# First layer norm of a Swin block without TensorE: 32x32 blocks transposed on VectorE, statistics spread through DRAM

## The reference

```python
xl = _ln(transpose(x, (0, 2, 3, 1)), norm1_w, norm1_b)        # over the 192 channels
xl = jnp.roll(xl, shift=(-3, -3), axis=(1, 2))
xw = windows of 7 x 7 tokens
q, k, v = xw @ qkv_w.T + qkv_b                                # 6 heads of 32
out = softmax(q @ k.T * 32 ** -0.5) @ v                       # in each window and head
out = out @ proj_w.T + proj_b
xl = roll back, then _ln(out, norm2_w, norm2_b)
h = gelu(xl @ fc1_w.T + fc1_b) @ fc2_w.T + fc2_b              # 768 hidden
return transpose(h, (0, 3, 1, 2)) + x
```

## Time and profile before

| | us |
|---|---|
| median of 3 runs | 3117.31 (3116.3 to 3117.31) |
| the profiled execution | 3117.07 |
| its span, first to last instruction | 3115.2 |
| PE busy | 3078.9 (99%) |
| DVE busy | 2490.3 (80%) |
| ACT busy | 2709.6 (87%) |
| POOL busy | 936.4 (30%) |
| mean granted TensorE clock | 0.996 |

### The profile page before, as it was taken

How to read it: one execution, slowest core, us unless ns; L and a number is a source line. 1 busy time by engine, 2 the same in 40 slices (tenths; PEclk the granted TensorE clock), 3 DMA queues, 4 the chain that set the end, 5 groups by cost and what they waited for, 6 DMA issues and landing times.

```text
span 3115.2 us, 77363 instructions
## 1 busy us (share of the span) xinstructions
PE 3078.9 (99%) x28076; PEld 2991.3 (96%) x28076; DVE 2490.3 (80%) x7339; ACT 2709.6 (87%) x5502; POOL 936.4 (30%) x1292
## 2 busy tenths in 40 slices
PE   6999999999999999999999999999999999999998
PEld 5999999999999999999999999999999999999998
DVE  6788788878888887788788878887888888878876
ACT  3988888888888888888888888888888888888887
POOL 1223322332233233323322332233223323332332
PEclk8999999999999999999999999999999999999999
DMA  3121112111221221122112211211221122112211
GB/s 69 31 45 43 39 40 45 42 38 41 43 43 39 42 47 39 39 44 44 38 40 44 44 38 40 46 41 39 41 47 39 38 42 47 39 39 44 44 29 28
DMA packets 458711, 129.33 MB, mean 42 GB/s; under 512 B 392803, under 2 KB 458084, under 8 KB 458340
## 3 DMA queue, kind: packets, MB, share of 16 engines
q1 hardware_dynamic: 455012, 122.71, 18.7%
q10 hardware_dynamic: 3328, 1.68, 0.2%
HBM read 47.20 MB, written 38.54 MB: 28 GB/s over the span
## 4 chain that ended last, share of the span: by engine, by line
PE 98%; SPq 1%; DVE 1%; ACT 0%; issue 0%; POOL 0%; DMA 0%; POOLq 0%; DVEq 0%; ACTq 0%
PE psum L311 8%; PE psum L313 7%; PE psum L312 7%; PE psum L314 7%; PE psum L315 7%; PE psum L593 6%; PE psum L568 6%; PE psum L548 5%; PE psum L549 4%; PE psum L559 4%; PE psum L550 4%; PE psum L560 4%; PE psum L574 4%; PE psum L518 4%; PE psum L321 3%; PE psum L323 3%
## 5 line engine op out<-in xcount | busy, mean ns | idle before, releaser
L926 DVE BATCH_NORM_STATS2 st<-psum 98x6 f32<-98x192 f32 x1024 | 354.7, 357 | 223.6 <-PE psum L495 223.5
L745 ACT ACTIVATE hh<-psum,b 128x392 fp32r<-128x392 f32 x768 | 451.5, 588 | 43.8 <-PE psum L315 29.2
L1133 POOL TENSOR_TENSOR ve<-mv,eps 98x4 f32<-98x4 f32 x256 | 80.1, 313 | 1290.2 <-DVE mv L932 1290.2
L748 ACT ACTIVATE hf<-psum,b 128x392 f32<-128x392 f32 x768 | 447.4, 583 | 0.0
L937 DVE TENSOR_SCALAR xn<-psum,mv,rs 98x192 f32<-98x192 f32 x1024 | 422.5, 466 | 6.3 <-POOL rs L1135 6.3
L977 DVE TENSOR_TENSOR hl<-hf,hh 128x392 fp32r<-128x392 f32 x640 | 350.6, 548 | 10.3 <-ACT hf L748 6.2
L1147 POOL TENSOR_TENSOR pr<-pr,rc 98x294 f32<-98x294 f32 x512 | 338.9, 681 | 17.6 <-DVE rc L1013 17.6
L708 ACT ACTIVATE pt<-psum 113x294 f32<-113x294 f32 x512 | 213.4, 417 | 125.1 <-PE psum L574 107.0
L548 PE MATMUL psum<-hh,w2h 128*128 128x392 f32 x768 | 286.4, 373 | 0.0
L311 PE MATMUL psum<-x_h,w_mh 128*128 128x392 f32 x768 | 281.1, 366 | 0.0
L1152 POOL TENSOR_TENSOR xt<-yr,xt 64x392 f32<-64x392 f32 x128 | 131.0, 1024 | 458.3 <-DVE yr L990 458.3
(11 more groups left out here) (137 smaller groups left out, 9980.7 us busy)
## 6 DMA issues: line engine op xcount, KB each, us to landing
vbd<-vs SPq DMA_DIRECT2D x1024, 36.8 KB
xt<-in_x SPq DMA_DIRECT2D x112, 194.5 KB, 2.7
out<-xt SPq DMA_DIRECT2D x112, 194.5 KB, 2.0
xt<-in_x SPq DMA_DIRECT2D x112, 97.2 KB, 2.4
out<-xt SPq DMA_DIRECT2D x112, 97.2 KB, 2.1
xt<-in_x SPq DMA_DIRECT2D x112, 48.2 KB, 2.2
xt<-in_x SPq DMA_DIRECT2D x256, 0.8 KB, 2.0
xt<-in_x SPq DMA_DIRECT2D x128, 1.5 KB, 2.2
```

The lines of the kernel that those rows point to most:

```text
L745: nc.scalar.activation(hh[:, m % HB, :], bank("fc1", m)[:, 0:T], ACT.Gelu, bias=b1[:, m:m + 1]).then_inc(s_hh, 1)
L748: nc.scalar.activation(hf[:, m % HB, :], bank("fc1", m)[:, 0:T], ACT.Gelu, bias=b1[:, m:m + 1]).then_inc(s_gelu, 1)
```

## The change

The first norm no longer uses PE.

- SP loads `x` a second time, in groups: `xg` holds channels modulo 32 in 32 partitions for each 128 tokens (`load_groups`, five DMAs for most units, six for the unit that wraps). The old load of the second half of the rest channels goes.
- DVE transposes 32x32 blocks of it (`token_blocks`, one instruction of 128x768) into `xtok`, tokens in partitions, and takes bn_stats and bn_aggr there. POOL's rstd goes into `mv[0]` beside the mean.
- SP writes mean and rstd to DRAM (`stats_out`) and reads them back into all partitions (`stats_in`), as `bc`.
- DVE (main channels) and POOL (rest) subtract the mean and multiply by rstd on the channel layout (`less_mean`, `times_rstd`), and ACT and DVE split from there.
- PE's transposes L493, L495 and the x1 ones of L518 go. Bias products move to PE's start.
- All pieces of all engines are placed anew, with other lags and banks.

The core of it:

```diff
+            def load_groups(u):
+                s_ = u % XG
+                if u >= XG:
+                    sp.wait_ge(s_tr, nth(u - XG, 1, 0))
+                for px, n, r, c in group_runs(u % UPB):
+                    sp.dma_start(xg[32 * r:32 * r + 32, s_, :, c:c + n],
+                                 xf[u // UPB, :, px:px + n].rearrange("(g c) n -> c g n", c=32)).then_inc(s_xg[s_], 16)
+            def stats_out(u):
+                sp.wait_ge(s_rs[0], nth(u, 1, 0))
...
+                sp.dma_start(spread_out[u % 2].rearrange("(p b) q -> p b q", b=PAIRS), mv[0][:, :, :]).then_inc(s_mr_out, 16)
+            def stats_in(u):
+                sp.wait_ge(s_mr_out, 16 * (u + 1))
...
+                sp.dma_start(bc[:, u % 2], spread_out[u % 2:u % 2 + 1].to_broadcast([128, T, 2])).then_inc(s_mr[u % 2], 16)
+            for t in range(UNITS + 7):
                 if t < UNITS:
+                    if t > 1:
+                        load_groups(t)
+                if 0 <= t - 2 < UNITS:
+                    stats_in(t - 2)
+                if 0 <= t - 4 < UNITS:
+                    spread(t - 4, 0)
+                    spread(t - 4, 1)
+                if 0 <= t - 1 < UNITS:
+                    stats_out(t - 1)
+                if 0 <= t - 7 < UNITS:
+                    store((t - 7) // UPB, (t - 7) % UPB)
+                    if t - 7 + AHEAD < UNITS:
+                        load((t - 7 + AHEAD) // UPB, (t - 7 + AHEAD) % UPB)
```

```diff
+            def token_blocks(u):
+                dve.wait_ge(s_xg[u % XG], 16 * sum(len(group_runs(v % UPB)) for v in range(u % XG, u + 1, XG)))
...
+                nc.vector.transpose(xtok.rearrange("p b (c d) -> p c b d", d=32),
+                                    xg[:, u % XG].rearrange("p c (t b) -> p c b t", b=PAIRS)).then_inc(s_tr, 1)
+            def less_mean(u, k):
...
+                nc.vector.tensor_tensor(ym1[:, :], xt[:, k, 0, :], bc[:, u % 2, :, 0], ALU.subtract).then_inc(s_ym1_sub, 1)
+            def times_rstd(u):
+                dve.wait_ge(s_ym1_sub, nth(u, 1, 0))
+                nc.vector.tensor_tensor(ym1[:, :], ym1[:, :], bc[:, u % 2, :, 1], ALU.mult).then_inc(s_ym1, 1)
```

More of the change, by code:

```diff
@@ L239, in runs, with group_runs @@
             return body + [(a - SHIFT, SHIFT, PB)]
[L241 to L248, removed]
+        def group_runs(i):
+            return [(px + c - at, min(n + at, c - c % 128 + 128) - c, c // 128, c % 128)
+                    for px, n, at in runs(i) for c in [at] + [z for z in range(128, T, 128) if at < z < at + n]]
         def transfers(i):
@@ L283, in last_read @@
                 return s_lo[name], v, 3, 2 * i
[L284 to L287, removed]
+            if name == "ln2":
+                return s_norm, v, PAIRS, 2 * i + 1
             if name == "vt":
@@ L302, in evicted @@
         def evicted(name, i, m):
-            ps = bank(name, i)[0:m, 0:T]
+            ps = (ym1, yr1)[i][:, :] if name == "x1" else bank(name, i)[0:m, 0:T]
             return ps.rearrange("p (r w c) -> p w r c", r=WIN, w=NW) if name == "x1" else ps
@@ L333, in x2_half_psum @@
             return bank("x2", 1)[CR * s:CR * (s + 1), 0:T // 2].rearrange("p (a b) -> p a b", a=WIN)
[L337 to L343, removed]
+        in_order = sorted(range(len(BANK_USES)), key=lambda k: (BANK_USES[k][3], k))
+        first_use = {}
+        for k in in_order:
+            first_use.setdefault(BANK_USES[k][2], (BANK_USES[k][0], BANK_USES[k][1]))
+        spare_0, spare_1 = list(first_use)[-2:]
         def qkv_columns():
@@ L472, in hidden_bias_products @@
[L472 to L482, removed]
-                    last = nc.tensor.matmul(ps, raw_1[1][0:CR, m * 128:(m + 1) * 128], nwb[0:CR, 7:8], start=False, stop=True)
-                last.then_inc(s_bias_mm, 1)
-                pe.wait_ge(s_bias, 3)
@@ L487, in to_tokens @@
-            def to_tokens(u, k, it, c):
-                if c == 0:
-                    pe.wait_ge(s_x[k], (it + 1) * loads(k))
-                claim(u, [("ln1", c)])
-                for q in (2 * c, 2 * c + 1):
-                    at = TP * tokens_of(q)
-                    nc.tensor.transpose(bank("ln1", c)[0:TP, main_of(q)], xt[:, k, 0, at:at + TP], ident[:, :])
-                nc.tensor.transpose(bank("ln1", c)[0:TP, CM:2 * CM], xt[:, k, 1, TP * c:TP * c + TP], ident[:, :]).then_inc(s_pe["ln1"], 1)
+            pe.wait_ge(s_small, SMALL)
@@ new lines, in step @@
+                if u[4] is not None:
+                    fc2_lo(u[4], 3)
+                    fc2_hi(u[4], 4)
+                    fc2_hi(u[4], 5)
+                    fc2_lo(u[4], 4)
+                if u[0] is not None:
+                    qkv(u[0], 4)
+                if u[4] is not None:
+                    fc2_lo(u[4], 5)
+                if u[3] is not None:
+                    fc1(u[3], 0)
+                if u[0] is not None:
+                    values(u[0], 0)
+                    values(u[0], 1)
@@ new lines, in step @@
+                if u[3] is not None:
+                    fc1(u[3], 1)
+                if u[2] is not None:
+                    project(u[2], 0)
+                if u[3] is not None:
+                    fc1(u[3], 2)
+                if u[2] is not None:
+                    project(u[2], 1)
+                    project(u[2], 2)
+                    project(u[2], 3)
+                if u[3] is not None:
+                    fc2_hi(u[3], 0)
+                    fc2_hi(u[3], 1)
+                if u[0] is not None:
+                    qkv(u[0], 3)
@@ new lines, in step @@
+                if u[3] is not None:
+                    fc2_lo(u[3], 0)
+                    fc1(u[3], 3)
+                    fc2_hi(u[3], 2)
+                if u[0] is not None:
+                    qkv(u[0], 2)
+                if u[3] is not None:
+                    fc1(u[3], 4)
+                    fc2_lo(u[3], 1)
+                    fc2_lo(u[3], 2)
+                    fc1(u[3], 5)
+                if u[0] is not None:
+                    values(u[0], 2)
+                    values(u[0], 3)
@@ new lines, in step @@
+                if u[6] is not None:
+                    hidden_lo(u[6], 3)
+                if u[5] is not None:
+                    normalise(1, u[5], 1)
+                    normalise(1, u[5], 2)
+                if u[3] is not None:
+                    v_out(u[3], 1)
+                if u[5] is not None:
+                    normalise(1, u[5], 3)
+                if u[2] is not None:
+                    lo_part("x1", u[2], 0)
+                if u[3] is not None:
+                    row_max(u[3], 0)
```

517 lines of the change are left out of this document (252 added, 265 removed), and 11 rows, old and new, of the table BANK_USES.

## The result

The changed kernel takes 3141.47 us (median of 4 runs, 3135.15 to 3141.91), the kernel before on the same chip 3116.81: ratio 1.0075, 95% interval 1.0063 to 1.0088. It is slower by 0.75%, where 3038 us was forecast, and outside the range 3005 to 3108.

A forecast was written before the change was run, and what follows sets the result against it. PE, full before, was to stall 0.85 us per step in a closed loop through the value moves: period 23.1 us, PE floor 22.25. Sum: 3115.2 - 125 x 0.76 + 16 (start) + 1.9 = 3038 us; range 3005 to 3108.

The forecast's parts named there:

- floor rival: Whole kernel: moves land earlier or finish_rest isn't late, so PE's floor of 22.25 us is reached, 2932 us; chance 0.08.
- third weighted: Start: the third unit's weighted matmuls, at 103.12 us before, placed at 119 after; +16 us, bounds 5 and 28.
- no slack elsewhere absorbs it: Loop weighted, SP's issues, landing, v_out, finish_rest, fc2_hi: closed, so PE's 0.85 us stall comes in each step.
- weighted to first issue: In each step, SP starts the eight value moves 1.69 us after weighted starts.
- first issue to `v_out`: SP and DMA: moves land 7.75 us after the first issue, plus 0.1 for the semaphore, 7.85 us.
- `v_out` to fc2_hi: DVE: copy, one bn_stats and finish_rest, then the semaphore, before PE gets fc2's bank; 1.40 us.
- fc2_hi to next weighted: PE's rest of the step after the stall: 22.25 - 10.1 = 12.15 us.
- PE's later needs: hidden_lo 1 and 2, second norm's rstd, row max: within 0.4 us of their turn; nothing taken, 0.3 us upper end.
- Another order wait adds: DVE's chain from v_out to less_max(1), or delayed landing: period 23.5 to 23.85 us, 3090 to 3115 us; chance 0.11.
- The stall lets the clock fall: PE: stall halves the clock in each step, products take 3 us more, period 26.1 us, 3415 us; chance 0.05.
- SP's queue becomes the loop: SP: 17.2 us plus five group loads, slower from 1.3 us each; 3240 us at 1.5; chance 0.07.
- The rule cited from the Trainium skill: 128x128 transposes: TensorE preferred to VectorE if the result may end in PSUM (390 ns against 311); not followed.

The follow-up runs named there:

- e1: The changed kernel with buffer `vs` twice, so `v_out` waits for the moves of the unit before the last: 2955.10 us, ratio 0.9482.
- e6: The changed kernel with two more small DMAs on SP between its wait for weighted and the eight moves: 3358.48 us, ratio 1.0775.
- e3: The changed kernel with group loads of x for the first three units only, later statistics stale: 3140.08 us, ratio 1.0074.
- e10: The changed kernel with the broadcast load of mean and rstd (`stats_in`) for two units only, later ones stale: 3132.34 us, ratio 1.0051.
- e4: The changed kernel with three of six column groups transposed on DVE after the first unit, statistics partly stale: 3134.34 us, ratio 1.0058.
- e2: The changed kernel with `finish_rest` moved ahead of `v_out` 0 in DVE's order, `vs` still single: 3068.95 us, ratio 0.9847.

## Why the prediction was wrong, point by point

**The mechanism was right.** PE waits before fc2_hi for DVE's `yr`, DVE waits before `vs` for the moves, and nothing else binds in the usual step. e1 gives the floor that was forecast, 22.38 for 22.25, and a total between the floor rival's 2932 and the forecast, at 2955; the rest of its distance to 2932 is 125 x 0.13 = 16 us of floor, 6 of start (e1's third weighted stands at 124.7 where 119 was forecast) and 2 of the end. The premise "no slack elsewhere absorbs it" is e6's one to one. What failed is the length of the loop.

**The size failed, in four terms.** The forecast span is 3036.1, the measured one 3139.5: 103 us.

| term | forecast | measured |
|---|---|---|
| weighted to first issue | 1.69 | 1.69 |
| first issue to `v_out` | 7.85 | 8.25 |
| `v_out` to fc2_hi | 1.40 | 1.49 |
| fc2_hi to next weighted | 12.15 | 12.32 |
| usual step | 23.1 | 23.75, median 23.73 |
| over it, long steps | 0 | 15.6 us in all |
| third weighted | 119 | 128.84 |

The measured terms are from the step at 1514 us above, by starts on the timelines, as the forecast took them: weighted begins there at 1514.08 and 1537.83.

1. *First issue to `v_out`, +0.4 us.* The forecast was 7.75 us to the end of the last DMA burst, read in slices of 0.1 us at one place, and 0.1 for the semaphore, for which it named no row. In the steady steps the eight issues take 6.79 us where that row had 6.59, so the last packet is over 7.98 us after the first issue instead of 7.75. From there to `v_out` it is 0.27 us, where 0.1 was put. So half of the miss is the issues and the other half the way from the last packet to the waiting instruction. I had called other traffic a rival ("can delay the landing"), but it isn't that: in the usual step nothing of note is in flight beside the moves, neither without the group loads (e3) nor without the broadcast (e10) is it shorter, and in the filling phase of the kernel after the same stretch took 8.15 us (87.50 to 95.65). Why the issues take 0.1 to 0.2 us longer than in the kernel before stays open.
2. *The rest of the step, +0.17.* Of it 0.13 is PE's floor, 22.38 where 22.25 was forecast. The rest is the first product after the stall, 0.25 us to the next start, where it is 0.20 in e1 without a stall. With the 0.09 of `v_out` to fc2_hi these are small terms, but all are multiplied by 125. Terms 1 and 2, taken by the median, are 23.73 - 23.1 = 0.63, times 125 = **79 us**, three quarters of the miss.
3. *No term for long steps.* Each step was taken alike. The 0.3 us of the range's upper end was meant for PE's later needs, not for issues or landings that are late now and then. A closed loop passes each of them on: of the **16 us** late landings are 5.0, slow or late issues 4.7 and the four falls of the clock behind them 6.3.
4. *The start, +10.* `stats_out(0)` is issued at 38.19 (forecast 38), and the first qkv starts at 53.54 (forecast 50); the hand-made order of the first steps, "by hand I place it at 119", was 10 short, within its bounds 5 and 28.

The sum of the terms is 79 + 16 + 10 = 105 against 103.

**Where the gain went.** PE's floor fell by 23.86 - 22.38 = 1.48 us, and the loop took back 23.73 - 22.38 = 1.35. The result is the small rest of two large terms, 0.13 us per step or some 16 us in all; the long steps eat that, and the start decides the sign. The prediction put a rest of 0.76 on a loop whose length it knew only from single rows. A miss of 3% in the loop's 23.1 us was enough; its own range for the period, 23.0 to 23.5, didn't have room for that.

**The rivals.** "Another order wait adds", 3090 to 3115, had the right period (23.5 to 23.85) by a wrong wait: PE never waits for DVE's less_max before weighted. Its time was also added up wrongly: by the forecast's own sum a period of 23.85 with +16 for the start is 3117 - 1 + 16 = 3132, not 3115, which belongs to 23.72. So this rival reached past no change at all into slower, and the prediction gave it no chance of that. "The stall lets the clock fall" had the right mechanism and was priced as all or nothing, at 3 us in every step: it happened in 4 steps here, at 1.57 us each, and in half of the steps once e6 had made the stall 0.8 us longer. "SP's queue becomes the loop" was wrong: five group issues took 2.52 us at 1509.14, 0.50 each (forecast 0.7, tipping point 1.2). The floor was reached as soon as the loop was open (e1).

**DVE.** The transpose of 128x768 takes 1.56 us (I took 1.1, with bounds 0.55 and 2.2), and subtraction and multiplication 0.56 and 0.53, as forecast. DVE as a whole was forecast at 19.6 us per step, 20.7 at worst; in e1, where the step is 22.38, it is busy for 21.4, partly because its instructions meet POOL's (hidden_lo, L1004, has a mean of 737 ns there and 624 in the kernel after; see below). The group in the kernel after:

```profile
L933 DVE STREAM_TRANSPOSE xtok<-xg 128x768 f32<-128x768 f32 x128 | 200.2, 1564 | 5.9 <-DMA xg<-in_x 5.9
```

By e4 this miss cost nothing. The rule cited from the Trainium skill ("VectorE: DVE Perf Modes", The three transpose paths), by which the change would lose, names a side that came out, but not its reason: in e1 the same transposes stand on VectorE and the kernel is 161 us faster than before. The measured price speaks the same way, 1.56 us on an engine with time free against 1.48 on the one that was full.

**POOL** was forecast at 1.02 us for each of its new operations; they take 1534 and 1347 ns, because they meet DVE operations. In the kernel after no steady wait of PE names them; in e2 the same meeting, the other way round, is what the step hangs on.

## What to carry over

Before work is taken from a full engine, list the loops that go across engines and through a DMA with single buffers and compute each one's length beside the new floor; if it is within a few per cent of the floor, either open it (a second buffer, or nothing urgent queued behind its wait) or measure each term up to the start of the instruction that waits, not to the last packet, and widen the range by the sum of the terms' errors times the number of steps. A step of a closed loop has no average to hide in: each late landing and each slow issue is paid in full. Time saved on an engine whose next instruction waits is not saved (e4), and a fixed cost at the start decides the sign when the rest is small.

## What the runs showed of the hardware

**DVE and POOL in each other's way.** The same 128x392 multiplication of two SBUF operands (`times_rstd`) takes 0.53 us alone and 1.36 when POOL's 64x392 operation of 1.04 us begins just ahead of it (e2, above). In e1 a hidden_lo meets two POOL operations in a row:

```profile
1505.99 2.08 DVE L1004 TENSOR_TENSOR hl<-hf,hh 128x392 fp32r<-128x392 f32 x1
...
1505.97 1.03 POOL L1186 TENSOR_TENSOR yr<-yr,bc 64x392 f32<-64x392 f32 x1
1506.97 1.64 POOL L1198 TENSOR_TENSOR pr<-pr,rc 98x294 f32<-98x294 f32 x2
```

2.08 us instead of 0.55: it grew by 1.53 us, more than the first of the POOL operations alone. POOL's turn isn't free either: L1182 has a mean of 1534 ns in the kernel after and of 1049 in e2, where it goes first. The Trainium skill ("SBUF — State Buffer", SBUF: two separate sides) says that VectorE with two SBUF inputs and GpSimd reading SBUF take turns, each for a whole instruction; the rows agree in size. I had counted nothing for it. POOL was busy for 7.3 us of a step before and is for 10.1 in e1.

**PE's clock fell after much shorter idle times than I had a row for.** The idle time before the first fc2 product in each step, and whether the granted clock was at 0.50 within the next 6 us:

| idle, us | after: fell / stayed | e6: fell / stayed |
|---|---|---|
| 0.5 to 1.3 | 0 / 103 | |
| 1.3 to 1.7 | 0 / 8 | |
| 1.8 to 2.1 | 2 / 0 | 24 / 45 |
| 2.1 to 2.5 | | 14 / 11 |
| 2.5 to 3.0 | 1 / 1 | 15 / 4 |
| over 3.0 | 1 / 0 | 3 / 0 |

The rows of before had only 0.73 us (stayed) and 2.97 (fell). In between it isn't a matter of this idle time alone: 1.99 us did either, and the longer it was, the more often the clock fell. In e10 it stayed after 13 idle times of 1.4 to 1.9 us. What else decides isn't shown by these runs.

**Equal issues and equal landings scatter.** The same eight moves reached `v_out` after 8.15 to 8.3 us in most steps. SP's eight issues, usually 6.7 to 6.8 us, took 7.0 to 7.5 in about one step of twelve, and the same issues were slow now and then in the kernel before (up to 7.2 us), where nobody waited for them. In the kernel after and in e1 some of these slow issues stand nine units apart, at the same units in both; in e3, with five issues fewer per unit, they stand eleven units apart. So these go with the program and not with chance; what they are isn't shown. Late landings after usual issues are rarer, 1.5 to 2.05 us and three in one trace. What delays them stays open too.
